# Narrow weights loaded in pieces, and a Fourier product computed from half of its matrix

## What is computed

```python
def real_fourier_orthogonal_multiply(c):      # n = 1024, along the last dim
    ...
    spectrum = jnp.concatenate(parts, axis=-1)
    return jnp.fft.irfft(spectrum, n=n, axis=-1).astype(c.dtype)
...
w0 = coefs0 * mask0.astype(coefs0.dtype)
w1 = coefs1 * mask1.astype(coefs1.dtype)
decoded = jnp.einsum('bsr,eor->ebso', e0, w0) + jnp.einsum('bsr,eor->ebso', e1, w1)
transformed = real_fourier_orthogonal_multiply(decoded)
update = transformed.sum(axis=0)
return base + update * SCALING                # SCALING = 0.5
```

## Time and profile before

| | |
|---|---|
| median of 3 runs | 1569.97 us |
| the 3 runs | 1573.96, 1569.97, 1569.53 us |
| the profiled execution | 1571.75 us |
| its span, first to last instruction | 1569.9 us |
| PE / DVE / ACT / POOL busy, share of the span | 97 / 55 / 50 / 22% |
| mean granted TensorE clock, share of full | 0.988 |

### The profile page before, as it was taken

One profiled execution on the slowest core, in us unless ns is written; L12 is line 12 of the kernel. 1 busy time (PEld: TensorE's weight loads), 2 busy tenths in 40 slices (PEclk: granted clock), 3 DMA queues, 4 the chain that ended last, 5 costly groups with the idle time before them and its releaser, 6 DMA issues.

```text
span 1569.9 us, 27470 instructions
## 1 busy us (share of the span) xinstructions
PE 1520.3 (97%) x7676; PEld 942.5 (60%) x7676; DVE 867.2 (55%) x2594; ACT 790.1 (50%) x1673; POOL 352.6 (22%) x210
## 2 busy tenths in 40 slices
PE   7879999989999999999999999999999999999998
PEld 2557777745556555666555555555556555666554
DVE  4645777885555555555555555555555555555554
ACT  4546666564444444444444444444444444444443
POOL 2645666511111111111111111111111111111110
PEclk9899999999999999999999999999999999999999
DMA  9586556343333322332332233333333332323221
GB/s 335 185 274 198 174 184 190 97 121 93 101 90 97 95 89 89 89 89 89 89 90 90 89 91 92 90 92 98 93 90 99 93 89 89 89 89 89 89 74 53
DMA packets 160533, 177.80 MB, mean 113 GB/s; under 512 B 104640, under 2 KB 123027, under 8 KB 160254
## 3 DMA queue, kind: packets, MB, share of 16 engines
q1 hardware_dynamic: 155974, 163.65, 34.4%
q10 hardware_dynamic: 4536, 13.89, 2.6%
HBM read 137.80 MB, written 39.32 MB: 113 GB/s over the span
## 4 chain that ended last, share of the span: by engine, by line
PE 83%; POOL 6%; issue 6%; DVE 3%; ACT 1%; DMA 1%; ACTq 0%; POOLq 0%; SPq 0%; DVEq 0%
PE pair L1349 42%; PE pair L84 7%; PE pair L85 7%; PE pair L86 7%; PE pair L1311 6%; POOL v_lo L244 6%; PE pair L1319 6%; PE pair L1285 2%; PE pair L446 1%; PE pair L1371 1%; PE pair L1370 1%; PE pair L1378 1%; PE pair L1300 1%; DVE m_lo L1405 1%; DMA fourier<-in_fourier 1%
## 5 line engine op out<-in xcount | busy, mean ns | idle before, releaser
L1349 PE MATMUL pair<-m_hi,t_x_hi 128*128 128x512 f16 x1024 | 306.4, 381 | 1.1 <-DVE m_lo L1405 1.1
L1349 PE MATMUL pair<-m_hi,t_x_lo 128*128 128x512 f16 x1024 | 305.0, 379 | 0.0
L1349 PE MATMUL pair<-m_lo,t_x_hi 128*128 128x512 f16 x1024 | 305.0, 379 | 0.0
L1186 POOL TENSOR_TENSOR t_narrow<-t_a_raw,t_narrow 128x256 f16<-128x256 f32 x64 | 43.9, 686 | 1046.7 <-ACT t_x_hi L1073 1046.7
L244 POOL TENSOR_TENSOR v_lo<-v_x,v_hi 128x1024 fp32r<-128x1024 f32 x64 | 154.9, 2422 | 113.6 <-ACT v_hi L238 113.4
L1349 PEld LDWEIGHTS pair<-m_hi,t_x_lo 128*128 128x128 f16 x1024 | 100.1, 98 | 121.3 <-issue 0.5
L1349 PEld LDWEIGHTS pair<-m_lo,t_x_hi 128*128 128x128 f16 x1024 | 100.1, 98 | 121.2 <-issue 0.6
L85 PE MATMUL pair<-t_narrow,t_x_hi 128*128 128x352 f16 x512 | 160.3, 313 | 0.0
L84 PE MATMUL pair<-t_narrow,t_x_hi 128*128 128x352 f16 x512 | 160.2, 313 | 0.1
L86 PE MATMUL pair<-t_narrow,t_x_lo 128*128 128x352 f16 x512 | 160.0, 313 | 0.0
L1140 ACT COPY t_out_sb<-pair 128x1024 f32<-128x1024 f32 x64 | 64.9, 1014 | 169.4 <-PE pair L1319 169.4
(11 more groups left out here) (248 smaller groups left out, 2850.5 us busy)
## 6 DMA issues: line engine op xcount, KB each, us to landing
v_x<-in_x SPq DMA_DIRECT2D x64, 512.0 KB, 3.5
t_xt<-in_x_t SPq DMA_DIRECT2D x64, 512.0 KB, 3.2
out<-t_out_sb SPq DMA_DIRECT2D x64, 512.0 KB, 2.7
t_rhs_b<-bk_hi SPq DMA_DIRECT2D x256, 64.0 KB, 2.3
t_a_raw<-in_lora_a SPq DMA_DIRECT2D x128, 64.0 KB, 2.9
t_bd<-w_kinds SPq DMA_DIRECT2D x128, 64.0 KB, 2.3
t_rhs_c<-bk_lo SPq DMA_DIRECT2D x128, 64.0 KB, 2.2
blk_raw<-in_left_blocks ACTq DMA_DIRECT2D x10, 512.0 KB, 4.7
```

What stands on the lines that cost most here:

```text
L1349: last = pe.matmul(pm_ps[:, c], lhs, m[:, k, c], start=a, stop=z)
```

## The change

**Fourier product.** A cosine row is even and a sine row odd about column 512. Only columns 0 to 512 of `fourier` are loaded (513 of 1024). The 40 summed columns get a second copy in which the sine rows are negated (a new input `sine_sign`, one DVE multiplication); it stands at columns 64 to 103 of a cleared tile `both` of 104 columns. A chunk is now one product 104 x 512 and one of a single column (column 512). Column 1024 - p of the result is column p of the mirrored copy: `cs_hi` and `cs_lo` are 104 rows, rows 0 to 39 filled in the left half and rows 64 to 103 in the right half (read in reversed order), the rest zeros by two memsets of POOL. `enc` is given twice, in rows 0 to 39 and 64 to 103. ACT's wait on the memsets is new.

**Narrow weights.** Seven loads (six of 512 KB, one of 256 KB) of `load_piece`, each but the first behind a wait for the one before; `square(j)` waits for piece j alone. Pieces and squares stand behind the rows named in `PIECES` and `SQUARES`; the key is (block, row). Since squares reach into blocks 4 and 5, these two are written out on ACT and its loop begins at block 6.

**Wvu** is loaded behind the load of block 2's raw data, at the end of setup, instead of ahead of row 2.

```diff
+    def cs_parts(cs):
+        return ((cs[0:RENC, LEFT], cs_ps[0:RENC, LEFT]),
+                (cs[MIRROR:EROWS, HALF:HALF + 1], cs_ps[MIRROR:EROWS, HALF:HALF + 1]),
+                (cs[MIRROR:EROWS, HALF + 1:HID], cs_ps[MIRROR:EROWS, HALF - 1:0:-1]))
...
+        sp.dma_start(sine_sign[:], t["sine_sign"]).then_inc(s["coefs_in"], 16)
...
-        act.dma_start(g["wvu_raw"][:], t["wvu"]).then_inc(g["wvu_in"], 16)
         rows_high(2)
         act.wait_ge(s["cs_mm_done"], 1)
-        act.mul(cs_hi[:], cs_ps[0:RENC, :], 0.5).then_inc(s["cs_hi_ready"], 1)
+        act.wait_ge(g["zeroed"], 2)
+        for out, src in cs_parts(cs_hi):
+            last = act.mul(out, src, 0.5)
+        last.then_inc(s["cs_hi_ready"], 1)
...
+        act.dma_start(g["wvu_raw"][:], t["wvu"]).then_inc(g["wvu_in"], 16)
         rows_high(9)
...
+        pool.memset(f(cs_hi[:]), 0.0)
+        pool.memset(f(cs_lo[:]), 0.0).then_inc(g["zeroed"], 1)
...
-            for c in (LEFT, RIGHT):
-                last = pe.matmul(cs_ps[0:RENC, c], coefs[:, 0, k * RENC:(k + 1) * RENC],
-                                 fourier[:, k, c], start=(k == 0), stop=(k == KC - 1))
+            for c in (LEFT, slice(HALF, HALF + 1)):
+                last = pe.matmul(cs_ps[0:EROWS, c], both[:, k, :], fourier[:, k, c], start=(k == 0), stop=(k == KC - 1))
...
-        dve.tensor_tensor(coefs[:, 0, :], coefs[:, 0, :], coefs[:, 2, :], ALU.add
-                          ).then_inc(s["wsum_ready"], 1)
+        experts = [coefs[:, n, :].rearrange("p (k r) -> p k r", r=RENC) for n in (0, 2)]
+        link(dve.tensor_tensor(both[:, :, 0:RENC], *experts, ALU.add))
+        sign = sine_sign[:].unsqueeze(2).broadcast_to([P, KC, RENC])
+        dve.tensor_tensor(both[:, :, MIRROR:EROWS], both[:, :, 0:RENC], sign, ALU.mult).then_inc(s["wsum_ready"], 1)
...
-    SQUARES = {2: (0, 1, 2, 3), 3: (4, 5, 6)}
+    PIECES = {(1, 2): 0, (1, 4): 1, (2, 1): 2, (2, 3): 3, (3, 1): 4, (3, 2): 5, (3, 4): 6}
+    SQUARES = {(2, 2): 0, (2, 4): 1, (3, 2): 2, (3, 4): 3, (LBLK, 1): 4, (LBLK, 3): 5, (LBLK + 1, 2): 6}
...
+        def load_piece(j):
+            if j:
+                act.wait_ge(s["w_all_in"], 16 * j)
+            else:
+                act.wait_ge(s["k_mm_done"], 2 * KC)
+                act.wait_ge(g["w_stored"], 16)
+            dst, src = piece(j)
+            act.dma_start(dst, src).then_inc(s["w_all_in"], 16)
...
-            act.wait_ge(s["w_all_in"], 48)
+            act.wait_ge(s["w_all_in"], 16 * (j + 1))
...
         store(LBLK - 1)
-        with act.Fori(0, KC // 2 - 1) as j:
+        one(LBLK, 0, evac_m(LBLK))
+        one(LBLK + 1, 1, evac_m(LBLK + 1))
+        with act.Fori(1, KC // 2 - 1) as j:
```

More of the change, by code:

```diff
@@ L53 @@
 RENC = 40
+MIRROR = 64
+EROWS = MIRROR + RENC
 NEXP = 3
@@ L292, in setup_stage @@
         coefs = tile(passing, "coefs", [P, NEXP, KC * RENC])
+        sine_sign = tile(passing, "sine_sign", [P, KC])
+        both = tile(passing, "both", [P, KC, EROWS])
         masks = tile(passing, "masks", [P, NEXP, KC * RENC // 4], I32)
@@ L295, in setup_stage @@
     with ExitStack() as early:
-        enc = tile(early, "enc", [RENC, HID], F32, "right")
-        enc_lo = tile(early, "enc_lo", [RENC, HID], F32R, "right")
-        enc_hi = tile(early, "enc_hi", [RENC, HID], F32R, "right")
-        cs_hi = tile(early, "cs_hi", [RENC, HID], F32R, "right")
-        cs_lo = tile(early, "cs_lo", [RENC, HID], F32R, "right")
+        enc = tile(early, "enc", [EROWS, HID], F32, "right")
+        enc_lo = tile(early, "enc_lo", [EROWS, HID], F32R, "right")
+        enc_hi = tile(early, "enc_hi", [EROWS, HID], F32R, "right")
+        cs_hi = tile(early, "cs_hi", [EROWS, HID], F32R, "right")
+        cs_lo = tile(early, "cs_lo", [EROWS, HID], F32R, "right")
         w_kinds = tile(early, "w_kinds_sb", [CH, NCOND, 4, CH], F32R, "right")
@@ L540, in vector @@
         dve.wait_ge(s["cs_hi_ready"], 1)
-        dve.scalar_tensor_tensor(cs_lo[:], cs_ps[0:RENC, :], 0.5, f(cs_hi[:]), ALU.mult,
-                                 ALU.subtract).then_inc(s["enc_cs_split"], 1)
+        for (out, src), (high, _) in zip(cs_parts(cs_lo), cs_parts(cs_hi)):
+            last = dve.scalar_tensor_tensor(out, src, 0.5, f(high), ALU.mult, ALU.subtract)
+        last.then_inc(s["enc_cs_split"], 1)
         rows_stats(1)
@@ L624, in row_hi, with beside @@
             var_hi(act, g, v, tile_of(b, q), q, (i + q) % 2, turn_of(b, q))
+        def beside(b, q):
+            if not isinstance(b, int):
+                return
+            if (b, q) in PIECES:
+                load_piece(PIECES[b, q])
+            if (b, q) in SQUARES:
+                square(SQUARES[b, q])
         def one(b, i, evac, last=False, old_rows=False):
@@ L630, in one @@
                 store(b - 1)
-            if isinstance(b, int) and b in SQUARES:
-                square(SQUARES[b][0])
+            beside(b, 1)
             row_hi(b, 2, i)
-            if isinstance(b, int) and b in SQUARES:
-                square(SQUARES[b][1])
+            beside(b, 2)
             if not last:
@@ L638, in one @@
             row_hi(b, 3, i)
-            if isinstance(b, int) and b in SQUARES:
-                square(SQUARES[b][2])
+            beside(b, 3)
             row_hi(b, 4, i)
-            if isinstance(b, int) and b in SQUARES and len(SQUARES[b]) > 3:
-                square(SQUARES[b][3])
+            beside(b, 4)
             if not isinstance(b, int) or b + 2 < NB:
@@ L667, in store, with piece @@
                 act.dma_start(t[part][b * P:(b + 1) * P, :], f(src)).then_inc(s["bk_stored"], 16)
-        def load_narrow_weights():
-            act.wait_ge(s["k_mm_done"], 2 * KC)
-            act.wait_ge(g["w_stored"], 16)
-            act.dma_start(s["a_all"][:], t["lora_a_k"].rearrange("k p n -> p k n")).then_inc(s["w_all_in"], 16)
-            act.dma_start(s["wu_all"][:], t["wu1_t"]).then_inc(s["w_all_in"], 16)
-            act.dma_start(s["wq_all"][:], t["wq_t"]).then_inc(s["w_all_in"], 16)
+        def piece(j):
+            if j < 4:
+                return s["a_all"][:, 2 * j:2 * j + 2, :], t["lora_a_k"][2 * j:2 * j + 2].rearrange("k p n -> p k n")
+            if j < 6:
+                return s["wu_all"][:, j - 4, :], t["wu1_t"][:, j - 4, :]
+            return s["wq_all"][:], t["wq_t"]
+        def load_piece(j):
[6 more added lines that the diff above has]
+            act.dma_start(dst, src).then_inc(s["w_all_in"], 16)
         def square(j):
@@ L687, in scalar @@
             if b == 1:
-                load_narrow_weights()
                 act.wait_ge(g["wvu_in"], 16)
@@ L1631, in fourier_matrix, with sine_sign @@
     return m.astype(np.float32)
+def sine_sign(n):
+    rows = np.arange(n)
+    return np.where((rows % 2 == 0) & (rows > 0), -1.0, 1.0).astype(np.float32)
 def kernel(**inputs):
@@ L1652 @@
     masks = np.concatenate([a["L1_ffn_mask0"], a["L1_ffn_mask1"]], axis=2).view(np.uint8)
+    enc = np.concatenate([a["L1_ffn_enc0"], a["L1_ffn_enc1"]], axis=0)
     def expert(m):
@@ L1676 @@
         "masks": np.ascontiguousarray(expert(masks)).view(np.int32),
-        "enc": np.concatenate([a["L1_ffn_enc0"], a["L1_ffn_enc1"]], axis=0),
-        "fourier": fourier_matrix(HID).reshape(KC, P, HID),
+        "enc": np.concatenate([enc, np.zeros((MIRROR - RENC, HID), np.float32), enc], axis=0),
+        "fourier": fourier_matrix(HID).reshape(KC, P, HID)[:, :, 0:HALF + 1],
+        "sine_sign": sine_sign(HID).reshape(KC, P).T,
         "w_base_t": a["L1_ffn_W_base"].T.reshape(KC, P, HID),
```

5 lines of the change are left out of this document (3 added, 2 removed).

## The result

| | before | after |
|---|---|---|
| median | 1570.98 us (4 runs, 1569.53 to 1573.96) | 1557.70 us (4 runs, 1556.42 to 1561.11) |
| profiled execution, its span | 1571.75, 1569.9 us | 1556.96, 1555.1 us |
| mean granted TensorE clock | 0.988 | 0.994 |

What follows compares the result with a forecast made beforehand. TensorE, busy 97%, bounds the kernel, so only its idling, lower clock or own work can yield time. Terms -11.4 -2.4 -1.1 -0.3 -5.2 +4.6 +2.4 = -13.4 gave 1558.3, carried to the median as 1556.6 us; 8-in-10 range 1547 to 1565.

Steps and rivals of the forecast that it cites:

- The burst's gap and clock: Fold block 2: loading narrow weights in pieces removes PE's 11.4 us gap and the half clock behind it, 2.4 us.
- The new wait: Block 3: piece 5 waits for piece 4, queued behind two stores; PE idles 4.6 us plus 2.4 of lower clock, costing 7.0.
- Block 4: Fold block 4: the store's wait ahead of row 1 remains; the later loop entry wins 0.3 us, 0 as other end.
- Setup: Before the fold blocks: shorter Fourier product and earlier start, less the longer cs_hi and cs_lo, win 5.2 us net.
- Product: PE's Fourier product in the setup: 16.45 us becomes 11.7, one-column records taken at 0.17 us each; 4.7 us saved.
- Start: PE's first Fourier product: half the bytes land sooner, then DVE's sums limit; start at 9.3 instead of 10.51, 1.2 us won.
- Row 3's load: Setup: 2.35 MB fewer bytes ahead of this load, at 366 GB/s, bring it 6.4 us earlier, enough to pass on 5.2.
- Wvu free: Wvu's load moved to the end of setup costs nothing: wanted a whole block later, against some 5 us to land.
- (1): Rival: in block 3 piece 4 is there in time, the 7.0 us are not paid; 1549.6; chance 0.18.
- (2): Rival: the setup gains nothing, by costly one-column products or short rows loading no faster; 1561.8; chance 0.13.
- (3): Rival: one further block, say block 2 on piece 2, waits with gap and clock drop, 3.6 + 2.4; 1562.6; chance 0.09.
- (4): Rival: every piece is slow, holding ACT with five clock drops, 35 us lost against 20.4 won; 1585; chance 0.05.

Runs made afterwards that it cites:

- piece_ahead_of_stores: The changed kernel with the piece behind row 1 of blocks 2 and 3 (pieces 2 and 4) issued ahead of the two stores; 1550.96 us.
- full_fourier: The changed kernel with the Fourier part undone (all 1024 columns, two 512-column products a chunk, enc of 40 rows), pieces and Wvu as changed; 1562.49 us, ratio 0.9938.
- x3_early: The changed kernel with SP's load of row 3 right behind that of row 2, ahead of row 2's picked W; 1555.42 us, ratio 0.9901.
- wvu_early: The changed kernel with Wvu loaded at its old place, at the start behind the small constants on ACT's queue; 1562.09 us, ratio 0.9928.
- full_load: The changed kernel with all 1024 columns of the Fourier matrix loaded, the products still reading 513; 1562.46 us, ratio 0.9940.
- piece5_later: The changed kernel with piece 5 issued behind row 3 of block 3 and piece 6 behind row 1 of block 4; 1552.09 us, ratio 0.9872.
- store_behind_row1: The changed kernel with the store of block 3's result placed behind row 1 of block 4 instead of ahead of it; 1556.64 us, ratio 0.9900.
- both_waits_gone: The changed kernel with the edits of piece5_later and store_behind_row1 together; 1549.87 us, ratio 0.9863.
- aligned_rows: The changed kernel with the half Fourier matrix's rows stored 576 floats apart instead of 513, as many bytes loaded; 1559.51 us, ratio 0.9929.

## Why the prediction was right, point by point

**What bounds the kernel: right.** All of the gain lies in PE's pauses and its clock in the fold, and in the setup. Block 5 keeps its length (18.80 us), though one of the squares now stands in it, and the span shrank by what block 5 starts earlier.

**The burst's gap and clock: right.** 11.4 + 2.4 = 13.8 us forecast, block 2 shrank by 13.75. Nothing else was late there: PE has no pause over 0.5 us in it. Of the six waits of one piece for another, one shows on PE.

**The new wait: right, by the mechanism forecast, with small errors that nearly cancel.** Piece 4 landed at S+11.1 (taken: S+10.5, within the bounds 8.7 to 11.4). Row 3 reached PE at S+18.1 (taken: 17.0). But PE also wanted it later, at 129.45 - 4.72 = 124.73, S+13.4 (taken: 12.5), in part since row 2 was late as well. The pause is 4.72 us against 4.6. The clock behind it cost less: twelve products in 4.55 us [the stretch above] are 1.8 over 12 x 0.23, not 2.4. On the other side, block 3's old pause ahead of row 2 was not gone, as the step on its two pauses has it (1.1 us): 0.48 us of the 0.58 stands there still. ACT was held by the stores and piece 4 (its square of row 2 begins 3.23 us after its last instruction, "issue"): 1.36 us of that are the wait ahead of the stores (1.09 before), and 1.87 the three issues. So **"I take nothing" for the issues' time was wrong**: one issue takes 0.35 to 0.76 us of ACT's queue, and here nothing hid it. Block 3 was forecast at 19.34 - 1.1 + 7.0 = 25.2 us and took 25.59.
One sentence of the step fell: that without the queue's order the stores wouldn't hold piece 4 up. The Trainium skill's "DMA: Bandwidth & Descriptors", section "Queues, rings and completion order", is not contradicted (bk_lo landed 4.6 us after its issue, at 119.5, piece 4 behind it at 122.4), but by piece_ahead_of_stores the way from issue to landing is only 0.9 us shorter without the stores ahead. Issued at S+4.2 with 6.0 us to landing, piece 4 would by this estimate still have been late, at S+10.2.

**Block 4: forecast 0.3 us, measured 1.67.** The store's wait stayed (4.27 for 4.70), PE's pause was 3.15 for 3.57, 0.42 us. The rest is the clock: it fell only 1.3 us after the pause's end, for ten products in 3.30 us, 1.0 over 10 x 0.23. By block 4 of before (24.72 us, 5.95 over block 1's 18.77 in the earlier trace rows, of which the pause is 3.57) a drop seemed to cost 2.4. Part of that varies from profile to profile: in seven profiles with this pause (3.14 or 3.15 us, the changed kernel's among them) the lower clock followed in five, and block 4 took 23.05 to 23.08 us; in two it didn't come at all (granted clock 1.00), and block 4 took 21.52. Why is not settled.

**Setup: the sum right (5.2, measured 5.48), its parts not.**
- Product: PE time 8.19 + 2.16 = 10.35 us, forecast 11.7. The term mis-sized most is that of the one-column records: the last eight records (four wide, four narrow) take 2.16 us, less 4 x 0.43 leaves 0.44, 0.11 each for the forecast's 0.17. That is 1.8 us for 2.7; the slow first records make the rest, 8.19 - 12 x 0.43 - 12 x 0.11 = 1.7 for 2.1. The prediction calls these records half clock; they go at half the pace, but the granted clock of that stretch is shown as 1.00, so the name isn't borne out. The weight load itself takes 0.168 us at least and 0.172 in the median [above], as taken from the earlier trace rows, but part of it lies under the neighbours. The Trainium skill's "TensorE: Matmul & The Clock Gate", section "LDWEIGHTS (loading the stationary operand)", gives by columns / 1.2 an estimate of 0.087 us; no record here is under 0.168. Its total of 1.4 us for the 16 records still lies nearer to the 1.76 measured (16 x 0.11) than my 2.7, probably because of that overlap.
- Start: 0.15 us won of the forecast's 1.2. The step took half the bytes to land 1.4 us sooner and DVE's chain to be the limit. But PE waited for the load, which landed 0.15 us sooner (10.36 for 10.51). With the signs' load gone DVE's chain is the limit (9.17); that load was priced at "a small one".
- Split: cs_hi and cs_lo take 1.25 and 1.46 us, 0.47 more; forecast 0.7.
- Row 3's load: "6.4 us, more than 5.2" **failed**. From the start until it landed, the queues had moved 334 GB/s x 36.2 us = 12.1 MB before and 290 x 33.7 = 9.8 MB after. So 2.3 MB had gone, as worked out (2.35), but they were divided by an unchanged rate. The rate fell: SP stood at its wait for the picked W until 12.02 us with the loads ahead already issued, and from 16 to 18 us the DMA engines ran half empty (share, GB/s: the last two). Before, that wait ended at 11.09. The change itself makes the difference: DVE starts 0.40 us later, behind the signs' load, and has one more operation (0.49 us) ahead of the picked W.

```profile
12.00:16.00 4.00, 4.00 (x13) 1.99 (x12) 2.35 (x2) 4.00 (x6) 0.35 (x1) 1.00 1.00 376
16.00:18.00 2.00, 2.00 (x9) 1.01 (x8) 0.00 (x0) 1.66 (x3) 2.00 (x2) 1.00 0.52 110
18.00:20.00 2.00, 2.00 (x11) 1.46 (x10) 0.00 (x0) 0.00 (x0) 2.00 (x2) 1.00 0.77 255
```

  SP issues row 3 at 22.02, later than before (21.38), behind picked W, W_base and a block. Fewer bytes ahead can't help a transfer that is not issued; they helped by 2.5 us through the shorter queue. And "that load was the limit" was true by 0.41 us only, ACT's idle time before it: the product's chain had ended just ahead of it, and in full_fourier it is the last to end. That the place counts is shown by x3_early, that the bytes count by wvu_early (through this load) and full_load (through the product). The idle stretch is not all of it: at an equal share the engines moved some 5% less (0 to 33.7 us: 338 GB/s at a share of 0.98 before, 290 at 0.89 after), and that remainder isn't settled.
- The rest goes with something that the prediction didn't name: the clock. Before, PE ran at the lower clock in parts of 35.8 to 59.7 us (0.79, 0.87 and 0.66 of full in the three stretches of 10 us from 30); after, only from 38.3 to 41.3 (0.90, 0.93, 1.00). What it is worth wasn't parted by a run; the table below shows how it goes with the start of block 1.
- "Wvu free": right that it isn't missed later; wrong that its move is a small part of 6.4 us. Without it the setup gains next to nothing.

**Rivals.** (1) Piece 4 in time: not so here, but true where it is issued one step earlier (`piece_ahead_of_stores`). Its price of 7.0 us was measured as 5.6 to 6.2. (2) The setup gains nothing, 1561.8: it didn't come, but each of full_load (1562.46), wvu_early (1562.09) and full_fourier (1562.49) gives its time, so it took little to bring it about. Of its reasons, one-column products cost much less than wide ones (0.11 for 0.43), but the half-size load did land hardly sooner. (3) and (4): no further wait reached PE; pieces took 7.6, 3.7, 7.8, 3.9 and 6.9 us (0 to 4) from issue to landing, under the 10.5 from which (4) decides.

The hit is thus partly luck. On the profiled executions the forecast was 13.4 us and the change is 14.85: setup 0.28 more than said, block 1 0.20, block 2 0.05 less, block 3 0.35 less, block 4 1.37 more. The medians say 13.3, because before's profiled execution lay 0.8 us over its median of four runs and after's 0.7 under.

Nor is one profile enough to call a term right to half a microsecond. In us, the clock as a share of full:

| run | block 1 starts | granted clock from 20 us to it | PE's pause ahead of row 3, block 3 | block 3 | block 4 |
|---|---|---|---|---|---|
| before | 79.07 | 0.88 | none | 19.34 | 24.72 |
| after | 73.59 | 0.97 | 4.72 | 25.59 | 23.05 |
| piece5_later | 72.57 | 1.00 | none | 19.37 | 23.08 |
| piece_ahead_of_stores | 74.31 | 0.94 | none | 18.90 | 23.05 |
| store_behind_row1 | 75.42 | 0.94 | 6.00 | 26.25 | 18.94 |
| both_waits_gone | 76.32 | 0.91 | none | 19.16 | 19.74 |
| aligned_rows | 74.62 | 0.94 | 6.21 | 26.42 | 23.08 |
| x3_early | 71.24 | 0.97 | 5.25 | 26.08 | 21.52 |
| full_fourier | 78.37 | 0.88 | 5.23 | 25.66 | 23.22 |
| full_load | 77.91 | 0.91 | 4.92 | 26.03 | 21.52 |
| wvu_early | 78.30 | 0.91 | 5.25 | 26.43 | 23.06 |

("None" is 0.30 us or less.) Wherever piece 5 waits for piece 4, block 3 is 25.59 to 26.43 us, 6.3 to 7.1 over before, where the sum had 5.9: the changed kernel's own profile is the lowest of the seven, and the step's error is up to 1.2 us, not 0.35.

## To carry to other kernels

In this kernel a wait for a transfer cost above all what stood ahead of the transfer's issue on the issuing engine: look there first, and issue small loads ahead of large stores, or put one more row of work between issue and wait, before making pieces smaller. When bytes are taken from a full load queue, don't divide them by the old rate; ask whether the issuing engine will have issued the next transfer by then, and follow every one of the paths into the consumer (here the Fourier product's chain and row 3's load, which ended within half a microsecond of each other), since shortening one alone may gain nothing. An edit's worth read from a sum of independent terms holds only while the limit stays the same.
